# A vision tower on one core: four groups of 8, 9, 9 and 6 images become groups of 6, 9, 9 and 8

## The reference

```
h = concat(class_token, patches(x) @ W_lin.T + b_lin) + position   # (32, 37, 256)
n = layernorm(h)
K = exp(n @ Wk);  V = n @ Wv;  Q = sigmoid(n @ Wq)
S = cumsum(K * V, axis=1) / (cumsum(K, axis=1) + 1e-6)             # over the 37 tokens
h = h + (S * Q) @ Wc
n = layernorm(h)
u = act_quant(n) @ weight_quant(w1).T                              # 256 -> 1024
u = silu(depthwise_conv1d(u, width 3, along the tokens))
h = h + act_quant(u) @ weight_quant(w2).T                          # 1024 -> 256
```

## Time and profile before

| | |
|---|---|
| Median of 3 runs | 188.48 us (188.04 to 189.65) |
| The profiled execution | 189.8 us; its span 188.0 us |
| Busy in the span: PE, DVE, POOL, ACT | 135.4, 133.8, 85.4, 80.6 us |
| Mean granted TensorE clock | 0.873 of full speed |

### The profile page before, as it was taken

One profiled execution on the slowest core, in us unless ns is written; L12 is line 12 of the kernel. 1 busy time (PEld: TensorE's weight loads), 2 busy tenths in 40 slices (PEclk: granted clock), 3 DMA queues, 4 the chain that ended last, 5 costly groups with the idle time before them and its releaser, 6 DMA issues. The chain is left out here.

```text
span 188.0 us, 2089 instructions
## 1 busy us (share of the span) xinstructions
PE 135.4 (72%) x672; PEld 110.1 (59%) x672; DVE 133.8 (71%) x265; ACT 80.6 (43%) x137; POOL 85.4 (45%) x97
## 2 busy tenths in 40 slices
PE   0585999895497799995999299289449924930851
PEld 0584777674475568894677199179249813920830
DVE  0044034039809759797769998988999999979892
ACT  0668700117800551385193136449625734571120
POOL 4010003999606726052709089252919246019190
PEclk9999999999669999999699859969956985585599
DMA  6999970000000000000000000000200001100003
GB/s 187 264 285 407 309 193 0 0 0 0 0 0 0 5 2 0 0 3 0 2 0 0 0 0 0 0 3 2 65 0 0 0 0 28 48 2 0 0 24 97
DMA packets 4566, 9.05 MB, mean 48 GB/s; under 512 B 910, under 2 KB 3340, under 8 KB 4428
## 3 DMA queue, kind: packets, MB, share of 16 engines
q1 hardware_dynamic: 4256, 8.70, 15.5%
q10 hardware_dynamic: 300, 0.23, 0.5%
HBM read 7.71 MB, written 1.21 MB: 47 GB/s over the span
## 5 line engine op out<-in xcount | busy, mean ns | idle before, releaser
L464 PE MATMUL pair<-linT,xT 128*111 128x256 f32 (+1 forms) x132 | 34.8, 424 | 2.8 <-issue 1.4
L464 PEld LDWEIGHTS pair<-linT,xT 128*111 128x111 f32 (+1 forms) x132 | 25.4, 197 | 10.4 <-ACT xT L661 1.7
L385 POOL TENSOR_TENSOR z<-x_flat,s_row 128x666 f32<-128x666 f32 (+1 forms) x12 | 17.9, 1522 | 18.5 <-ACT s_row L739 18.5
L698 ACT ACTIVATE y<-pair,cb_sb,cw_sb 128x333 f32<-128x333 f32 (+2 forms) x32 | 17.4, 597 | 16.0 <-PE pair L506 16.0
L320 POOL TENSOR_TENSOR rstd<-var,minus_half 111x3 f32<-111x3 f32 x8 | 7.8, 970 | 32.0 <-DVE var L843 32.0
L506 PE MATMUL pair<-xq_hi,w1T 128*128 128x334 f32 (+2 forms) x64 | 19.4, 394 | 2.3 <-DVE xq_lo L906 2.3
L830 DVE TENSOR_TENSOR h<-pair,pos_sb 111x256 f32<-111x256 f32 (+1 forms) x11 | 4.4, 402 | 20.7 <-PE pair L464 20.7
L506 PE MATMUL pair<-xq_lo,w1T 128*128 128x334 f32 (+2 forms) x64 | 17.6, 364 | 0.0
L918 DVE SCALAR_TENSOR_TENSOR y<-pair,cw_sb,y 128x324 f32<-128x324 f32 (+2 forms) x32 | 15.1, 510 | 2.9 <-ACT x_flat L709 2.5
L506 PEld LDWEIGHTS pair<-xq_hi,w1T 128*128 128x128 f32 x64 | 14.5, 260 | 3.0 <-DVE xq_lo L906 2.6
L866 DVE RECIPROCAL krec<-ksum 128x333 f32<-128x333 f32 (+2 forms) x8 | 15.8, 1986 | 0.0
(11 more groups left out here) (112 smaller groups left out, 283.1 us busy)
## 6 DMA issues: line engine op xcount, KB each, us to landing
x_flat<-in_x_dram SPq DMA_DIRECT2D x6, 576.0 KB, 12.0
z<-in_L_ffn_w_dram SPq DMA_DIRECT2D x1, 1024.0 KB, 11.9
y<-in_L_ffn_w_dram SPq DMA_DIRECT2D x1, 1024.0 KB, 14.0
out_dram<-o_sb SPq DMA_DIRECT2D x10, 96.0 KB, 1.7
lin_sb<-in_L_tok_W_lin_dram SPq DMA_DIRECT2D x1, 768.0 KB, 4.9
wk_sb<-in_L_attn_Wk_dram SPq DMA_DIRECT2D x1, 256.0 KB, 10.5
wv_sb<-in_L_attn_Wv_dram SPq DMA_DIRECT2D x1, 256.0 KB, 10.6
wq_sb<-in_L_attn_Wq_dram SPq DMA_DIRECT2D x1, 256.0 KB, 10.4
```

The costliest lines, as they stand in the source:

```text
L385: nc.gpsimd.tensor_tensor(z_of[f][:, 2 * i:2 * i + 2, :], act_of[f][:, 2 * i:2 * i + 2, :], s_row[:, :T[f]].unsqueeze(1).to_broadcast([P, ...
L464: last = nc.tensor.matmul(ps[:n, j % 2, :D], xT[:, k, FIRST[g] * L + t0:FIRST[g] * L + t0 + n], linT[:, k, :], start=(k == 0), stop=(k == ...
L698: nc.scalar.activation(y(f)[:, k, :], pair(("f1", f, i))[:, b, :T[f]], ACT.Identity, bias=cb_sb[:, k:k + 1], scale=cw_sb[:, k, 1:2]).then_ ...
```

## The change

The first and the last group change places in size. Group 0 now has 6 images in two tiles, group 3 has 8 in three tiles. The groups start at images 0, 6, 15 and 24 in place of 0, 8, 17 and 26.

```diff
-    SIZES = [8, 9, 9, 6]
+    SIZES = [6, 9, 9, 8]
     assert sum(SIZES) == B
     G = len(SIZES)
     FIRST = [sum(SIZES[:g]) for g in range(G)]
```

## The result

The changed kernel takes **191.94 us** (median of 4 runs, 191.31 to 193.31) against 188.66 us for the kernel before beside it (188.04 to 189.65): a ratio of 1.018, interval 1.013 to 1.023. The forecast was 185.6, so the sign is wrong. The profiled execution took 193.31 us with a span of 191.1, and its span is 3.1 us longer than before. It is the slowest of the four. A ratio here compares, for each kernel, only the executions within 1.5% of its fastest, so it is not the quotient of the medians, and where the two part the text gives both.

What follows compares the result with a forecast made beforehand. DVE was taken to bound the kernel after 95.4 us, and before that how early group 2's products begin. Head -9.4 and dense part +6.5 made -2.9 from 188.48, so 185.6 us, range 182.8 to 189.2.

Steps and rivals of the forecast that it cites:

- the head: From the start to DVE's product of group 2 at 95.42 us: 9.4 us gained, ends 7.3 and 11.5.
- the dense part: From group 2's product to the end of the kernel: 6.5 us added, ends 4.8 and 8.4.
- From there to 95.4 PE is nearly always at work: From embed(1, 2)'s end to group 2's product: narrower chunks, shorter copies and missing transposes on PE gain 1.5 us.
- a sign of being wrong: At group 1's k: a granted PE clock of 0.50 there would show the forecast wrong.
- Regrouping: POOL's regrouping of x: starts near 38.4 and ends near 43.5 against 47.95, 4.4 us earlier.
- The wait ahead of `embed(1, 2)`: On PE, 1.38 us of waiting for ACT's copies of x's second half: goes, and nothing takes its place.
- rival 3: The wait ahead of embed(1, 2) stays because PE's order is unchanged: 1.4 us lost, 187.0; chance 0.07.
- I take 48.0: End of embed(1, 2) on PE, 55.87 before: 47.2 at full clock to 50.1 at low; 7.9 us gained.
- Rival 1: PE's clock falls at group 1's k and v, +1.9 to +2.2 us each: some 189.9 in all; chance 0.12.
- Group 0's attention chain on DVE and POOL is hidden: In the head: it lies behind POOL's regrouping and embed(1, 2); 0.9 us less on PE only lengthens a pause.
- The wait for the sum at 110.08: Group 1's first chunk on PE waits for DVE's sum, then near 109.3: -0.5 us taken, +0.8 at low level.
- Another sign of being wrong: Group 1's first chunk starts over 2 us after the scales' transposes, and DVE idles there by more than 1.

Runs made afterwards that it cites:

- e2_warm: Changed kernel with unread transposes filling PE's holes from the second half of x to group 1's k; 187.64 us, 0.990 of the kernel before.
- e1_clip: Changed kernel with DVE's clipping of the second weight matrix moved behind group 0's token scales; 190.93 us, 0.998 of the kernel before.
- after: The changed kernel, groups of 6, 9, 9 and 8, first measurement and profile; 191.94 us, 1.018 of the kernel before.
- after_again: The changed kernel unaltered, measured and profiled a second time; 191.83 us, 1.015 of the kernel before.
- e3b_6996: Changed kernel with the last group cut to 6 images, two images left out, run again for a usable profile; 181.14 us, 0.959 of the kernel before.
- e7_tailwarm: Changed kernel with 18 unread transposes on PE ahead of group 3's last products; 191.81 us, 1.013 of the kernel before.
- e10_add_first: Changed kernel with DVE's sum for group 3's second tile put ahead of the reciprocal it stood behind; 189.64 us, too scattered for a ratio.
- e14_add_first_again: Changed kernel with DVE's sum for group 3's second tile ahead of the reciprocal, run again; 188.95 us, 1.000 of the kernel before.
- before: The kernel before the change, groups of 8, 9, 9 and 6; 188.66 us beside the changed kernel.
- e13_before_add_first: Kernel before with DVE's sum for group 3's second tile put ahead of the reciprocal; 186.24 us, 0.988 of the kernel before.
- e5_early: Changed kernel with embed(1, 2) early, ahead of PE's second-half x transposes, its sum behind group 0's running sums, clipping moved; 187.02 us, 0.991 of the kernel before.
- e8_before_warm: Kernel before with unread transposes filling PE's holes in the head; 188.55 us, 0.988 of the kernel before.
- e6_7997_early: Groups of 7, 9, 9, 7 with embed(1, 2) ahead of the second half's transposes and the clipping moved; 191.80 us, 1.020 of the kernel before.

## Why the prediction was wrong

**The sum.** In the first profile the head gave 5.1 us where 9.4 were forecast, and the dense part with the end cost 8.1 where 6.5 were: 4.3 of the 6.0 us of the miss are the head's. In the second they are 5.9 and 6.8, and the head has nearly the whole of it.

**The step that failed** is the one from `embed(1, 2)` to the products: *"From there to 95.4 PE is nearly always at work"*, priced at 1.5 us of gain, with group 1's k at the full clock it had before. In its place the stage from `embed(1, 2)` to group 1's product grew by 3.7 us in the first profile and 3.0 in the second. Of these, 1.3 us stand ahead of the k in both, nearly all of it the collision of `hn` with the clipping, and 2.3 and 1.6 are the k at the low level, which the forecast had named as a sign of being wrong. Filling PE's holes brings the k back to 2.51 us (e2_warm), and moving the clipping brings `hn` back to 1.64 (e1_clip).

**The head, step by step.** Regrouping is right (ends 43.25; 43.5 forecast), though by another way: both running sums still met POOL's instructions (2.23 and 2.27 us for 444 columns; 2.53 for the 592 of the earlier trace rows), and even 12 columns of L852 took 1.05. The wait ahead of `embed(1, 2)` went: right, rival 3 is out. Its end is right in one execution and wrong in the other: *"With no hole ahead of it PE should regain its level sooner: I take 48.0."* (The 2.6 us taken there for twelve matmuls at full clock are 2.75 in its row, which moves this bound by 0.15.) In the first profile PE's transposes had holes until 43.30, it fell at 42.8, and nearly the whole of `embed(1, 2)` ran low, to 50.02, the bound of 50.1 that the text had named. In the second PE fell at 39.6 and was back at 46.4, and `embed(1, 2)` ended at 48.25. The kernel was slower than before both times, so this step alone does not explain the sign.

**Rival 1 came about, in part.** Group 1's k at the low level: 2.3 and 1.6 us more, where that rival had 1.9 to 2.2; its v ran at full clock. It is no accident of one execution: in all seven profiles of kernels with the change's order in the head and no fillers there (after, after_again, e1_clip, e3b_6996, e7_tailwarm, e10_add_first, e14_add_first_again) the k took 4.1 to 4.8 us, in the two of the kernel before without fillers (before, e13_before_add_first) 2.48. The pause that the rival named is not the cause by itself: filling the holes brings the level back (e2_warm), and so does an order with a longer pause further ahead (e5_early), while taking away 1.1 us of waiting does not (e1_clip). The rival was worth more than 0.12. The clock of this stretch before, 1.00 in spite of the pauses ahead of k, was taken as a property of the work, but the low stretch moved when PE's holes some microseconds earlier did. Which hole decides, no run shows. The Trainium skill, "TensorE: Matmul & The Clock Gate", Part 1, has it that the gate's default is the throttled state and that activity releases it; both filler runs agree, where more work for PE made the kernels 2.5% and, less surely, 1.2% faster.

**A cost that was not in the sum: the collision.** *"Group 0's attention chain on DVE and POOL is hidden"* was read for its length, not for what it would meet. With a tile less, DVE comes to the clipping 0.5 us earlier against POOL's `hn`; before, it started at 61.63, just when `hn` had ended. Now it lay inside, and `hn` took 2.73 us: 1.1 us on the path, as e1_clip shows. The Trainium skill, "GPSIMD Engine Reference", section 1, says that GpSimd shares its SBUF interfaces with VectorE and contends with DVE's instructions of two SBUF inputs or in a two-port mode; the trace agrees that the two contend (1.62 us alone, 2.73 beside 1.21 of clipping), and shows how much: nearly the whole length of the other instruction.

**Better than forecast**: from group 1's product to group 2's, 2.9 us in place of 1.5 with all in it, because group 2's k ran at full clock in this execution, and had run low before. First the kernel before, then the change:

```profile
88.97 4.17 PE L482 MATMUL pair<-hnT,wk_sb 128*128 128x333 f32 x8 [1.99 <-ACT hnT L668]
```

```profile
85.57 2.48 PE L482 MATMUL pair<-hnT,wk_sb 128*128 128x333 f32 x8 [1.84 <-ACT hnT L668]
```

This is luck: in the second profile of the change it ran low (3.93 us), the stage gave 1.2, and that execution's span was still 2.2 us shorter.

**The dense part.** The added work was priced well: up to `xq_lo` +3.3 (+2.2 in the second profile) for 3.0, +0.5 for 1.2, +1.8 for 1.7, SP +1.1 for 0.9. Two terms were mis-sized. The wait for the sum at 110.08: the chunk starts 14.2 us after group 2's product, near the 13.9 forecast, but at the low level, where DVE's taps come 0.6 later; the text knew this case as +0.8 and took -0.5. The profile showed only 3.39 us of idle PE ahead, and I asked what the wait would add, not what it already cost: some 2 to 3 us in both kernels. Another sign of being wrong, at this wait, came half: PE idled 2.43 us ahead of the chunk, but DVE's two waits behind it were 0.5 and 0.9. And the 24 last matmuls, taken at 0.1 more, cost 1.2 and 0.9 in the two profiles at the low level; at full level 0.1 would have been right (e7_tailwarm: 0.8 where 0.7 was before). Whether the median feels it stays open.

**What stays open.** Two executions of the changed kernel differ by 2.2 us in span (191.1 and 188.9); by the table this lies where low stretches fall on other instructions, so that each stage's figure is uncertain by one or two us, and there is one profile of the kernel before, from an execution 1.3 us above its median. With PE's holes in the head filled in both (e2_warm, e8_before_warm) their ratios agree within the intervals, but the clock was not made equal; with the sum moved in both they differ by 1.2%. The loss is not split more finely than that. Whether the early order would also help 8, 9, 9, 6 wasn't tried, since there group 1 needs the second half of x.

## What to carry to other kernels

A stage that starts earlier is worth its time only if the work behind it has the same clock and the same neighbours: before pricing a gain, look in the trace for what each later instruction of another engine would then lie beside, and take stretches at PE's low level as a cost that moves with PE's holes, not one that goes with the instruction. Moving work from a loose stage to a tight one is a poor trade unless the order is changed to use what the smaller first stage makes possible; here the exchange alone cost 1.5 to 1.8%, and with the early order, the moved clipping and the moved sum the kernel is 3.6% faster than before. And a wait that two kernels share is invisible in their difference: test a repair on the kernel before too.

## What the runs showed that was not expected

- Transposes that nobody reads made PE's stretch from 40 to 60 us run at a granted clock of 1.00 and the kernel 2.5% faster than the change without them (2.2% by the medians).
- One short DVE instruction can wait for a whole one of POOL: 12 columns (L852) took 1.05 us at 36.40 in the changed kernel, until POOL's rounding of the second weight matrix (L399, 35.52 to 37.42) had ended; 18 columns take 0.18 elsewhere. A running sum of 518 columns took 3.82 us beside POOL's regrouping (e6_7997_early), one of 444 took 2.23.
- The level of group 1's k (4.8 us low, 2.5 full) is not told by the pause ahead of it: 0.95 us in the kernel before, in the change and in the early order alike.
- The low stretches of one kernel do not stand still: in two executions of the change they began at 42.8 and 56.4, and at 39.6 and 53.3, and `embed(1, 2)` took 4.91 and 3.55 us.
